# GpSimd instead of VectorE normalises x in most layers of a four-layer hybrid kernel

## The reference

```python
def _layernorm(x, axis=-1, eps=1e-05):
    m = jnp.mean(x, axis=axis, keepdims=True)
    v = jnp.var(x, axis=axis, keepdims=True)
    return (x - m) / jnp.sqrt(v + eps)
...
x = x + _L0_attn_a_ref(_layernorm(x, axis=-1), ...)
x = x + _L0_ffn_ref(_layernorm(x, axis=-1), ...)
x = x + _L0_attn_b_ref(_layernorm(x, axis=-1), ...)
x = x + _L0_ffn_ref(_layernorm(x, axis=-1), ...)
```

## Time and profile before

| | before |
|---|---|
| time, median of 3 runs | 966.35 us (965.08 to 968.86) |
| the profiled execution: its span, the one time the page has for it | 965.1 us |
| PE busy | 890.3 us (92%) |
| DVE busy | 733.7 us (76%) |
| ACT busy | 533.5 us (55%) |
| POOL busy | 381.6 us (40%) |
| mean granted PE clock | 0.975 |

### The profile page before, as it was taken

How to read it: one execution, slowest core, us unless ns; L and a number is a source line. 1 busy time by engine, 2 the same in 40 slices (tenths; PEclk the granted TensorE clock), 3 DMA queues, 4 the chain that set the end, 5 groups by cost and what they waited for, 6 DMA issues and landing times.

```text
span 965.1 us, 20229 instructions
## 1 busy us (share of the span) xinstructions
PE 890.3 (92%) x6766; PEld 696.7 (72%) x6766; DVE 733.7 (76%) x2379; ACT 533.5 (55%) x1410; POOL 381.6 (40%) x554
## 2 busy tenths in 40 slices
PE   5779998989999999978999999999999997999996
PEld 4656776767767776656878888788878776777763
DVE  6668888889889887664766767685867677889973
ACT  6545454543445454526667575757575762554555
POOL 2468788876535443351212112020202000444445
PEclk9789999999999999989999999999999999999999
DMA  6432333331113655001202020202112021132321
GB/s 199 61 54 56 54 45 55 54 55 36 35 35 68 134 109 132 2 16 41 45 1 45 1 44 2 45 2 45 23 23 45 1 34 33 38 62 47 73 48 35
DMA packets 51287, 46.63 MB, mean 48 GB/s; under 512 B 6624, under 2 KB 48624, under 8 KB 51184
## 3 DMA queue, kind: packets, MB, share of 16 engines
q1 hardware_dynamic: 51184, 45.34, 23.4%
HBM read 11.40 MB, written 2.10 MB: 14 GB/s over the span
## 4 chain that ended last, share of the span: by engine, by line
PE 35%; DVE 12%; issue 4%; ACT 1%; DMA 1%; POOL 0%; SPq 0%; POOLq 0%; ACTq 0%; DVEq 0%
PE bank L285 9%; PE bank L1928 5%; PE bank L1878 5%; PE bank L1936 4%; PE bank L1866 3%; DVE weights L1442 3%; DVE q_lo L1422 2%; PE bank L1701 2%; DVE weights L1432 2%; PE bank L1713 2%; DVE arena L1270 1%; PE bank L1698 1%; PE bank L1739 1%; ACT oT L944 1%; DVE rope L1420 1%
## 5 line engine op out<-in xcount | busy, mean ns | idle before, releaser
L1270 DVE TENSOR_REDUCE arena<-bank 128x2 f32<-128x512 f32 (+1 forms) x192 | 128.9, 679 | 27.8 <-PE bank L1701 27.3
L886 ACT ACTIVATE weights<-bank 128x512 f32<-128x512 f32 x144 | 85.7, 596 | 115.4 <-PE bank L1713 114.4
L965 ACT ACTIVATE weights<-weights,neg_max 128x128 f32<-128x128 f32 (+1 forms) x256 | 113.8, 449 | 19.4 <-DVE neg_max L1432 19.4
L1432 DVE CUSTOM_DVE_ANT_0 weights<-bank,arena 128x128 f32<-128x128 f32 (+1 forms) x256 | 80.9, 353 | 56.6 <-PE bank L1928 54.8
L696 POOL TENSOR_SCALAR_AFFINE_SELECT weights<-weights 128x256 f32<-128x256 f32 x144 | 68.3, 475 | 127.4 <-ACT weights L886 127.3
L972 ACT ACTIVATE weights<-bank 128x384 f32<-128x384 f32 x128 | 62.7, 490 | 85.6 <-PE bank L1936 83.4
L1701 PE MATMUL bank<-kf_stack,q_stack 96*128 96x128 f32 (+1 forms) x512 | 109.8, 317 | 0.0
L1928 PE MATMUL bank<-kbT,arena 128*128 128x128 f32 (+1 forms) x512 | 105.1, 328 | 1.1 <-DVE y L420 0.9
L648 POOL TENSOR_SCALAR weights<-weights 128x512 f32<-128x512 f32 x64 | 97.3, 1530 | 13.4 <-ACT weights L789 13.1
L1442 DVE TENSOR_SCALAR weights<-weights,inv_sum 128x128 f32<-128x128 f32 (+1 forms) x256 | 83.8, 370 | 4.5
L285 PE MATMUL bank<-x_hi,wb_hi 128*128 128x256 f32 x256 | 83.4, 326 | 2.8 <-DVE q_lo L1422 2.8
(11 more groups left out here) (232 smaller groups left out, 2412.0 us busy)
## 6 DMA issues: line engine op xcount, KB each, us to landing
q_stack<-q_hi SPq DMA_DIRECT2D x96, 128.0 KB, 3.8
arena<-arena SPq DMA_DIRECT2D x64, 128.0 KB, 2.5
q_stack<-q_lo SPq DMA_DIRECT2D x48, 128.0 KB, 4.0
ka_stack<-k_hi SPq DMA_DIRECT2D x32, 76.5 KB, 3.6
x_all<-x SPq DMA_DIRECT2D x8, 256.0 KB, 5.1
st_wo<-b_wo SPq DMA_DIRECT2D x8, 256.0 KB, 3.9
arena<-b_wqn SPq DMA_DIRECT2D x8, 256.0 KB, 3.4
out<-x_all SPq DMA_DIRECT2D x8, 256.0 KB, 2.1
```

The source lines that it names most:

```text
L886: a.activation(s["pT"][(STEPS * b + k) % N_PT], p2[k % 2][:, :], ACT.Exp).then_inc(s["exp"], 1)
L965: last = a.activation(p, p, ACT.Exp, scale=-1.0, bias=neg_max[:, h % 4, t:t + 1], accum_out=sums[:, h % 4, t:t + 1])
L1270: v.tensor_reduce(into, p1[k % 2][:, :].rearrange("p (h k) -> p h k", h=n), AX.X, ALU.max, negate=True).then_inc(s["maxed"], 1)
L1432: last = v.tensor_tensor_reduce(out=probs[:, h % 4, part], in0=ps_s[h % 2][:, part], in1=mask_b[:, (1 - t) * P:2 * P], scale=1.0, scalar=F ...
```

## The change

POOL computes `neg_mean` beside `rstd`, for every layer and batch. For batches 2 to 7 of attention a and all batches of both ffn layers it also writes `xn`, as (x + neg_mean) * rstd, two instructions of 128x256. DVE keeps that work for batches 0 and 1 of attention a and for attention b. POOL does it at the end of step 8 in attention a and in step 4 of ffn, behind that step's `guard` or `causal`. `dve_stats` gets a wait on the previous `xn`, since `mv` and `rstd` are single buffers now read by POOL.

```diff
+        neg_mean = sb("neg_mean", [P, NT])
...
         def dve_stats(s, b):
 
             v = nc.vector
+            v.wait_ge(*(at(s, "xn", b, 0) if b or s is sa else at({"f": sa, "b": sf[0], "g": sm}[
+                "g" if s is sf[1] else s["kind"]], "xn", B - 1, 1)))
...
             g.tensor_scalar(var_eps[:, :], mv[:, :, 1], EPS_LN, None, ALU.add).then_inc(s["rstd"], 1)
-            g.wait_ge(*at(s, "rstd", b, 1))
+            g.tensor_scalar(neg_mean[:, :], mv[:, :, 0], -1.0, None, ALU.mult).then_inc(s["rstd"], 1)
+            g.wait_ge(*at(s, "rstd", b, 2))
             g.tensor_tensor(rstd[:, :], var_eps[:, :], expo[:, :], ALU.pow).then_inc(s["rstd"], 1)
...
+        def pool_normalize(s, b):
+            g = nc.gpsimd
+            g.wait_ge(*at(s, "rstd", b, 3))
+            wait_xn_read(g, s, b)
+            for t in range(NT):
+                last = g.tensor_scalar(xn[:, t, :], x_tile(b, t), neg_mean[:, t:t + 1], rstd[:, t:t + 1],
+                                       ALU.add, ALU.mult)
+            last.then_inc(s["xn"], 1)
...
+                if k == 8 and b >= 0 and there(b + 2):
+                    pool_normalize(sa, b + 2)
...
+                    if k == 4 and there(b + 2):
+                        pool_normalize(s, b + 2)
...
-                if k == 9 and there(b + 2):
+                if k == 9 and b < 0 and there(b + 2):
                     dve_normalize(sa, b + 2)
...
-                    if k == 5 and there(b + 2):
-                        dve_normalize(s, b + 2)
```

More of the change, by code:

```diff
@@ L142, in signals @@
         def signals(layer, kind, **own):
-            per = dict(stats=4, rstd=2, xn=1, xT=1, x_hi=1, x_lo=1, x_done=1, **own)
+            per = {**dict(stats=4, rstd=3, xn=1, xT=1, x_hi=1, x_lo=1, x_done=1), **own}
             return dict(kind=kind, per=per, past=0, **{n: sem(f"{layer}_{n}") for n in per})
@@ L310, in pool_rstd, with wait_xn_read @@
             g.tensor_scalar(var_eps[:, :], mv[:, :, 1], EPS_LN, None, ALU.add).then_inc(s["rstd"], 1)
-            g.wait_ge(*at(s, "rstd", b, 1))
+            g.tensor_scalar(neg_mean[:, :], mv[:, :, 0], -1.0, None, ALU.mult).then_inc(s["rstd"], 1)
+            g.wait_ge(*at(s, "rstd", b, 2))
             g.tensor_tensor(rstd[:, :], var_eps[:, :], expo[:, :], ALU.pow).then_inc(s["rstd"], 1)
+        def wait_xn_read(eng, s, b):
+            if s is not sa and b == 0:
+                eng.wait_ge(*at(sa if s is sf[0] else sf[0] if s is sm else sm, "xT", B - 1, 1))
+            else:
+                eng.wait_ge(*at(s, "xT", b, 0))
+        def pool_normalize(s, b):
[6 more added lines that the diff above has]
+            last.then_inc(s["xn"], 1)
         def dve_normalize(s, b):
             v = nc.vector
-            v.wait_ge(*at(s, "rstd", b, 2))
-            if s is not sa and b == 0:
-                v.wait_ge(*at(sa if s is sf[0] else sf[0] if s is sm else sm, "xT", B - 1, 1))
-            else:
-                v.wait_ge(*at(s, "xT", b, 0))
+            v.wait_ge(*at(s, "rstd", b, 3))
+            wait_xn_read(v, s, b)
             for t in range(NT):
```

## The result

| | before | after |
|---|---|---|
| median, us | 965.72 (4 runs, 963.57 to 968.86) | 977.2 (4 runs, 976.07 to 977.67) |
| ratio, 95% interval | | 1.0123 [1.0102, 1.0143] |
| span of the profiled execution, granted PE clock | 965.1, 0.975 | 974.3, 0.969 |

The forecast was 975.0 (range 964 to 985), +8.5 on the profiled execution. The sum was close, but several of its terms were not, and their errors cancelled; that part was luck, and what follows is mostly about it.

A forecast was written before the change was run, and what follows sets the result against it. POOL, then ACT, were taken to set PE's transpose in the first attention, DVE being only equally late. Terms 6.7 + 0.3 + 2.3 - 0.8 = +8.5 on the profiled 965.1 gave 973.6, about 975 us as median; range 964 to 985.

The forecast's parts named there:

- What sets the transpose (POOL, then ACT): First attention, batches 3 to 7: PE's transpose of x follows POOL's q_f by way of ACT; DVE is only equally late.
- PE's waits for DVE are the real ones: Rival, step 11 of the first attention: PE's wait for DVE binds, so the kernel gets faster, about 959.6 us; chance 0.10.
- The pair, 1.80 us: POOL's two normalising instructions per batch, taken at 0.90 us each from a line between L310 and L648.
- The rough estimate of 0.8 us: POOL's pair by the skill's 769 ns for 512 elements; set aside because L648 took 1530 ns for 512 columns.
- about 3.6 us behind q_f: First attention, five batches: where the profile would show PE's transpose starting if the forecast was right.
- Batches 3 to 7, +6.7: First attention: neg_mean, guard and pair on POOL make each of five transposes 1.34 us later.
- neg_mean, +0.22: First attention: the small POOL instruction ahead of q_f counts whole in the chain PE waits for; elsewhere free.
- Batch 2, +0.3: First attention, batch without a guard: transpose at 46.98 us instead of 46.67; range 0 to 1.5.
- q_lo's lateness costed at nothing: First attention: q_lo and its DMAs come 2.0 us later, their PE users 1.34; the remaining 0.7 us costs nothing.
- Steady feed-forward batches, +2.3: Nine batches: POOL's pair pushes its mask onto DVE's L1293, +0.26 us each; DVE's relief gains 0.
- The overlap, -0.8: Where first attention and feed-forward overlap: DVE's relief gains at most 1.7 us, half taken because guards crowd POOL.
- The clock: Part of the much slower rival (chance 0.17): longer waits double PE's low-clock stretch, 1.7 us per batch, 8.4 in all, 983.

The follow-up runs named there:

- before_exp4: Kernel before the change with ACT's copy q_hi moved from step 8 to step 11, only in first-attention rounds 3 and later; 962.63 us, ratio 0.9971.
- ffn_only: Changed kernel with the first attention as before (DVE normalises, no neg_mean there), POOL normalising only in the feed-forward layers; 968.34 us, ratio 1.0023.
- attn_only: Changed kernel with the normalisation of both feed-forward layers back on DVE, neg_mean kept everywhere; 975.0 us, ratio 1.0086.
- overlap_dve: Changed kernel with only batches 0 and 1 of the first feed-forward layer normalised on DVE again; 975.21 us, ratio 1.0102.

## Why the prediction was right or wrong, point by point

- **What sets the transpose (POOL, then ACT): right.** PE's wait for DVE fell and came back as waits for ACT and POOL; the kernel got slower, so the rival "PE's waits for DVE are the real ones" is out. `before_exp4` adds to it: the gain was in q_hi's place on ACT.
- **The pair, 1.80 us: too much.** It takes 1.09. Adding the columns' cost of L648 was the faulty step: a maximum over 128x512 in place says little of add-and-multiply. The rough estimate of 0.8 us worked out in the prediction from the Trainium skill (GPSIMD Engine Reference, section 3.1) was nearer than my row: 1.09 against 0.8 and 1.80. For a transpose I foretold "about 3.6 us behind q_f"; my own sum had 152.62 - 149.21 = 3.41, and it is 2.70.
- **Batches 3 to 7, +6.7: +6.4 in the profiled execution (7.88 - 1.45), by another sum, and so by luck.** Per batch +0.50, +2.29, +0.54, +1.42, +1.68. From q_f to the transpose it is +0.41 in each (2.70 against 2.29), 2.1 in all, where I had +1.12 and 5.6. The other 4.4 lie ahead of q_f, where I had 5 x 0.22 = 1.1. In the last batch q_f comes 1.27 us later after the transpose: 0.80 of it is there when `var_eps` starts, 0.69 of that from PE's matmuls at the lower clock, and 0.47 follow, from `neg_mean` and from a `var_eps` of 0.50 in place of 0.22, less a shorter `rstd`. In batch 4 it is 1.88 later, 0.82 of that beside DVE's long subtraction. The rest of the 4.4 is not taken apart.
- **neg_mean, +0.22:** 0.23 long, 0.31 with the gap behind it, in the chain as I said. That the form it allows takes less than half the time of the other I did not know.
- **Batch 2, +0.3:** +0.56 from batch 1 to 2 in this profile, within a start that varies by more.
- **q_lo's lateness costed at nothing: right.** In the first 250 us PE waited once for q_lo's DMA, 0.9 us after and 1.4 before; for POOL's x_lo it waited 1.5 us after and 1.0 before.
- **Steady feed-forward batches, +2.3: wrong, 0.** 19.20 us as before. The step that failed is the end of the pair. With my 1.80 it would have ended at 324.84 and the mask behind it at 325.5, across DVE's L1317 (the former L1293); it ends at 324.14:

```profile
323.04 1.10 POOL L333 TENSOR_SCALAR xn<-x_all,neg_mean,rstd 128x256 f32<-128x256 f32 x2
324.09 0.64 POOL L718 TENSOR_SCALAR_AFFINE_SELECT weights<-weights 128x512 f32<-128x512 f32 x1
325.04 0.19 DVE L1317 TENSOR_TENSOR arena<-arena 128x32 f32<-128x32 f32 x1
328.22 0.27 PE L1746 MATMUL bank<-cst,arena 128*16 128x128 f32 x1 [0.36 <-DVE y L440]
```

  The mask now ends at 324.73, 0.3 us ahead of L1317, and PE waits for DVE's quotients as before: DVE's relief gave nothing, as said.
- **The overlap, -0.8: wrong in sign.** Batches 7 to 9 (178 to 233 us before) lost 3.8 us in the profile (`ffn_only` 3.95, `attn_only` 0.9), 1.4 came back by batch 12. I had read the relief of DVE from two rows and left POOL's list there, where the pair stands ahead of k_lo, at "I take half"; and the clock's fall with a longer wait was only a rival's.
- **The clock:** priced in a rival at up to 1.7 us a batch. In the middle batches the stretch at the lower clock grew by 0.2 us in all, so that rival is out; in the overlap it is 2.95 us of the forecast's own case.
- **The sum.** In the profile: 0.9 to batch 1, 0.56 to batch 2, 6.4 to batch 7, 3.8 to batch 9, -1.4 to batch 12, -2.3 to batch 17 and +1.2 to the end, +9.2 against a forecast of +8.5. Steady feed-forward batches were 2.3 too high and the overlap 3.2 too low; the two errors nearly cancel, and the -2.3 is no effect of the change that any run shows.

## What to carry to other kernels

Before moving work off an engine that PE is seen to wait for, ask what the next instruction in PE's list waits for: here a second chain ended at the same point, and it ran through the very engine that received the work. Where an engine's list is gapless over the stretch that matters, an instruction put into it moves all that stands behind it by its whole length, and its mean share of busy time (40% here) tells nothing of that. What this costs depends on which place behind it is waited for: ahead of the guard the pair cost 4.7 us less than behind it. The cheap gain was in the order: a copy that waits (q_hi) stood ahead of short ones that did not have to.

## What the runs showed of the hardware that I had not expected

- POOL's tensor_scalar on 128x256 in float32, two operations, per-row operands: 0.557 us with add and multiply, 1.22 us with subtract and multiply (medians of 44 each). The maximum with a constant over 128x512 takes 1.52. Whether it is the subtraction, or the mean's place in `mv` (every second element), was not separated.
- Two two-input operations that overlapped in time, one on POOL (128x512) and one on DVE (128x1056), took 2.10 and 2.26 us in place of 1.28 and 1.24; DVE's had begun inside the POOL operation ahead. The rows fit the exclusive lock that the Trainium skill describes (SBUF — State Buffer, "Who interferes with whom").
- Idle matmuls kept PE's granted clock at 1.00 through the middle batches (0.91 to 0.94 without). In the kernel before they gave 2.6 us from batch 5 to batch 8, and it was 4.56 us late at batch 3.
- Where two waits of PE in the overlap were 1.37 and 1.31 us long, the granted clock fell, and the instructions up to the next transpose took 7.07 us; with a single wait of 1.07 there they took 4.12. `ffn_only` repeats the first (1.37, 1.32 and 7.17), `overlap_dve` the second (1.06 and 4.12).
- The same instructions reach batch 2 at 45.73 us in one execution (`attn_only`) and at 48.31 in another (`overlap_dve`), 2.6 us apart. What decides it stays open.
